# Expert rows by accumulating scatters instead of two fetched planes, in a two-layer graph and mixture-of-experts kernel

## The chip, the cores and the metric

The kernel runs on one core of one Trainium2 chip. The metric is the device time of one execution in microseconds (us), as the median of several runs. The core has five engines with queues of their own: TensorE (PE, and PEld for its weight loads), VectorE (DVE), ScalarE (ACT), GpSimd (POOL) and SyncE (SP), and 16 DMA engines that they share.

## What is computed

The reference adds four blocks to a residual `x` of 8192 tokens (64 groups of 128, in 4-byte floats) with 128 features each:

```
x = x + gnn0(layernorm(x))     # graph filter in the eigenbasis of the Laplacian
x = x + ffn0(layernorm(x))     # 8 experts, each token goes to 2 of them
x = x + gnn1(layernorm(x))     # graph filter with two batch norms
x = x + ffn1(layernorm(x))     # a shared expert, and 8 private ones, 2 of them for each token
```

Each of the two expert layers gives a token a weighted sum of two experts' rows:

```
gates = einsum('nk,nke->ne', topk_probs, onehot)
out   = einsum('ne,nec->nc', gates, y)
```

## The kernel before, in words

The code numbers the expert layers 0 and 1. The text calls them the first and the second one.

`X` holds the residual in SBUF, one partition for 64 tokens (token = 64 * partition + q), and is worked on in 16 slices of 4 values of q (512 tokens, 256 KB). Each layer of experts has two phases.

- Routing runs inside the graph stage before it. GpSimd scatters each token's normalized row twice, once for each expert chosen, into `rows` (`xs` in the code) in memory, with the gate and the token's number in two more columns (`Router.scatter`, L868).
- The experts then work on tiles of 256 rows of one expert. There are always `NT` = 71 tiles for each layer: 16384 rows, and padding of whole tiles. SyncE loads a tile (`experts_sp`, L1139), TensorE turns it, multiplies and turns it back in two halves of 128 rows, ScalarE writes half 0 times its gate to `ysb` (L1223) and VectorE half 1 (L1184). GpSimd sends each half to memory with one indirect DMA (`experts_pool`, L1150), so there are 142 of them for each layer. `ysb` has three buffers: both writers wait, for tile j, until the two scatters of tile j-3 have landed (`tile_back0` to `tile_back2`).

The destinations are in `goal`. It is filled with `NOWHERE`, a row that lies outside, and VectorE copies the token's number over it for real rows (L1172), so padding rows are dropped. In the number a token's second choice counts 8192 more than its first, so the two rows of a token land in two planes of 4 MB each (`planes`). No two scatters write the same bytes, and none waits for another.

After the last tile SyncE waits for all scatters and fetches the planes slice by slice into eight buffers (`fetch_planes`, L1329), and VectorE adds the two pieces to `X` (`add_planes`, L1338 and L1340). After the first expert layer this is the head of each step of `mix_dve`, in front of the layer norm sums (L926) of the next graph stage. After the second layer it is `last_dve`, and `last_store` on GpSimd writes each finished slice to `out` (L1642).

The order of the work is written by hand for each engine, and semaphores tie the engines together. SyncE's queue has, in this order: the loads of the start, the tile loads of the first layer, the second layer's weights (4.6 MB, L1765 and L1766, once the last tile of the first layer has copied its weights), the planes, the tile loads of the second layer, and the planes again.

Of the kernel before, what the change touches and what calls it, by code (L numbers as in the profile page):

```python
# [5 lines left out]
F32 = mybir.dt.float32  # L6
# [6 lines left out]
N = 64  # L13
# [671 lines left out]
ROW = P + 2  # L685
NOWHERE = 1 << 20
WB = (2 * HID0 + 3 * P, 2 * CH1 * P + CH1 + 2)
# [69 lines left out]
class Router:  # L757
# [115 lines left out]
    def table(self, dve, own):  # L873
# [187 lines left out]
def gnn0_dve(nc, dve, own, S, t, ps, route):  # L1061
    V, X = nc.vector, t["X"]
    dve.wait_ge(S("cleared"), 16 * BLOCKS)
    for s in range(A0_STEPS):
# [27 lines left out]

def clear_rows(nc, pool, S, zeros, xs):
# [7 lines left out]
    pool.wait_ge(S("cleared"), 16 * BLOCKS)  # L1101


def gnn0_pool(nc, pool, S, t, route, xs):
    for k in range(2):
        nc.gpsimd.iota(t["payi"][k][:, :, P], pattern=[[1, N]], base=k * TOKENS, channel_multiplier=N
                       ).then_inc(S("ids"), 1)
    pool.wait_ge(S("ids"), 2)

    def ready(g):  # L1110
        pool.wait_ge(S("a0_dup"), 2 * g + 2)
    for g in range(GROUPS):
        route.scatter(pool, g, xs, ready)


def uses(slot, ways):

    return len(range(slot, NT, ways))
# [23 lines left out]

def experts_pool(nc, pool, S, t, layer, planes):
# [174 lines left out]

def fetch_planes(sp, S, t, planes, layer, used):


    for w in range(3):
        sp.wait_ge(S(f"tile_back{w}"), 32 * uses(w, 3) * (layer + 1))
    rows = planes.rearrange("(k p q) c -> k p q c", k=2, p=P)
    for T in range(TILES):
        if T >= 8:
            sp.wait_ge(used, T - 7)
        for k in range(2):
            sp.dma_start(t["yb"][T % 8][:, k, :, :], rows[k][:, T * PAIRS:(T + 1) * PAIRS, :]  # L1329
                         ).then_inc(S(f"plane{T % 8}"), 16)  # L1330


def add_planes(V, dve, S, t, layer, T, done):

    xt = t["X"][:, T * PAIRS:(T + 1) * PAIRS, :]
    yb = t["yb"][T % 8]
    dve.wait_ge(S(f"plane{T % 8}"), 64 * layer + 32 * (T // 8 + 1))
    V.tensor_tensor(xt, xt, yb[:, 0, :, :], ALU.add).then_inc(done, 1)  # L1338
    dve.wait_ge(done, 2 * T + 1)
    V.tensor_tensor(xt, xt, yb[:, 1, :, :], ALU.add).then_inc(done, 1)  # L1340
    dve.wait_ge(done, 2 * T + 2)

# [272 lines left out]
def gnn1_pool(nc, pool, S, t, route, xs):  # L1615
    pool.wait_ge(S("bn2_ready"), 1)
    for k in range(2):
        nc.gpsimd.iota(t["payi"][k][:, :, P], pattern=[[1, N]], base=k * TOKENS, channel_multiplier=N
                       ).then_inc(S("ids"), 1)
# [8 lines left out]
def last_dve(nc, dve, S, t):  # L1628
    V = nc.vector
    for T in range(TILES):  # L1630
        if T == 0:
            dve.wait_ge(S("a1_xsh"), TILES)
        add_planes(V, dve, S, t, 1, T, S("z_add"))
        V.nop().then_inc(S("z_used"), 1)


def last_store(pool, S, t, out):

    for T in range(TILES):
        qs = slice(T * PAIRS, (T + 1) * PAIRS)  # L1640
        pool.wait_ge(S("z_used"), T + 1)
        pool.dma_start(out[:, qs, :], t["X"][:, qs, :]).then_inc(S("stored"), 16)  # L1642
    pool.wait_ge(S("stored"), 16 * TILES)


def build(nc, d, out, scratch):

    with ExitStack() as ctx:
# [8 lines left out]
        xs, planes = scratch  # L1657
        ps = [ctx.enter_context(nc.psum_tensor(f"bank{i}", [P, 512], F32)) for i in range(8)]
# [18 lines left out]
        t["OUT1"] = U1[:, :]  # L1677
        t["yb"] = [U1[:, w * 2 * TOK:(w + 1) * 2 * TOK].rearrange("p (k q c) -> p k q c", k=2, q=PAIRS) for w in range(8)]
        t["WS"] = W[:, E8 * WB[1]:E8 * WB[1] + WSH]
# [72 lines left out]
        def _(sp):  # L1752
# [8 lines left out]
            sp.dma_start(K[:, :], d["kroute"]).then_inc(S("kroute_in"), 16)  # L1761
            sp.dma_start(W[:, 0:E8 * WB[0]], d["w0"]).then_inc(S("w0_in"), 16)
            experts_sp(nc, sp, S, views[0], 0, xs)
# [3 lines left out]
            fetch_planes(sp, S, t, planes[0], 0, S("m_used"))  # L1767
            experts_sp(nc, sp, S, views[1], 1, xs)
            sp.wait_ge(S("a1_t1"), TILES)
            fetch_planes(sp, S, t, planes[1], 1, S("z_used"))  # L1770

# [14 lines left out]
        def _(dve):  # L1786
# [15 lines left out]
            experts_dve(nc, dve, own, S, views[1], ps, 1)  # L1802
            last_dve(nc, dve, S, t)

# [12 lines left out]
        @block.gpsimd  # L1817
        def _(pool):
            clear_rows(nc, pool, S, PAY[:, 0:ZERO], xs)
            gnn0_pool(nc, pool, S, t, routes[0], xs)  # L1820
            experts_pool(nc, pool, S, views[0], 0, planes[0])
            gnn1_pool(nc, pool, S, t, routes[1], xs)
            experts_pool(nc, pool, S, views[1], 1, planes[1])
            last_store(pool, S, t, out)

# [46 lines left out]
```

## Time and profile before

| what | value |
|---|---|
| median of 3 runs | 1550.68 us (1549.52 to 1550.79) |
| profiled execution, device time | 1551.85 us |
| its span, first to last instruction | 1550.1 us |
| busy: PE, DVE, ACT, POOL | 72%, 57%, 48%, 36% |
| mean DMA rate over the span | 81 GB/s |
| mean granted TensorE clock | 0.918 of full speed |

The profile is of one execution. Line numbers are those of the kernel before. Busy shares are means over stages with different limits: the stretches in which TensorE is full are those of the two expert layers, and the last 42 us have no TensorE work in them. Times to landing count from the start of the issuing instruction to the last update of the DMA's semaphore.

### The profile page before, as it was taken

What the parts mean: (1) busy time and instruction counts of PE and PEld (TensorE: products, weight loads), DVE (VectorE), ACT (ScalarE), POOL (GpSimd) and SP (SyncE); (2) the same over time, 40 slices, a digit from 0 to 9 for tenths busy, and PEclk for the clock granted to TensorE, in tenths of its full rate; (3) what the DMA queues carried; (4) which work ended last, traced back from release to release, by engine and by line L of the source; (5) the groups of instructions that cost most, each with busy time, mean ns of one, the idle gap of its engine ahead of it and who ended that gap; (6) DMA issues with size and microseconds to landing.
All of it is one profiled execution on the core that took longest, in us unless ns stands there. A gap on an engine that the chain in (4) does not pass through costs nothing.

```text
span 1550.1 us, 22393 instructions
## 1 busy us (share of the span) xinstructions
PE 1122.8 (72%) x5462; PEld 855.4 (55%) x5462; DVE 881.3 (57%) x3280; ACT 743.1 (48%) x2097; POOL 564.5 (36%) x575
## 2 busy tenths in 40 slices
PE   3445478028873049999999766859999499999970
PEld 3444467025652037777777533345554388888860
DVE  5555578866886026666666488686652233333325
ACT  3777748103451013443344367627775266666640
POOL 2000000000777744444444400006777455555543
PEclk9999999999895569999999989959999699999995
DMA  9991000000111111122222450001111122222218
GB/s 236 428 430 70 2 1 1 0 0 1 48 52 52 48 48 59 58 62 61 59 59 63 161 203 1 0 1 46 52 53 49 52 69 67 69 68 64 67 54 309
DMA packets 59120, 124.86 MB, mean 81 GB/s; under 512 B 13116, under 2 KB 39620, under 8 KB 57456
## 3 DMA queue, kind: packets, MB, share of 16 engines
q0 software_dynamic: 20000, 73.21, 12.7%
q1 hardware_dynamic: 38992, 50.23, 11.3%
q8 instruction: 45, 0.74, 0.2%
q14 instruction: 83, 0.68, 0.1%
HBM read 50.22 MB, written 74.99 MB: 81 GB/s over the span
## 4 chain that ended last, share of the span: by engine, by line
PE 57%; DVE 17%; ACT 8%; issue 7%; POOL 7%; DMA 3%; SPq 1%; DVEq 0%; POOLq 0%; ACTq 0%
PE bank L1289 14%; PE bank L1281 8%; POOL rows L868 7%; PE bank L1278 6%; PE bank L1279 6%; PE bank L366 3%; PE bank L1487 2%; PE bank L1480 2%; PE bank L181 2%; PE bank L1266 2%; PE bank L1300 2%; PE bank L1454 2%; DMA u<-planes 1%; ACT work L1394 1%; PE bank L1415 1%
## 5 line engine op out<-in xcount | busy, mean ns | idle before, releaser
L1150 POOL DMA_INDIRECT planes<-pay,goal x284 | 288.0, 1014 | 328.6 <-DVE pay L1184 152.5
L868 POOL DMA_INDIRECT rows<-pay,slot x256 | 252.1, 985 | 384.9 <-issue 348.7
L1289 PE MATMUL bank<-pay 128*128 128x256 f32 (+1 forms) x994 | 269.4, 388 | 0.1
L1167 DVE COPY pay<-wreg 128x1066 f32 (+1 forms) x142 | 111.7, 787 | 253.0 <-ACT pay L1249 107.0
L1289 PEld LDWEIGHTS bank<-pay 128*128 128x128 f32 (+1 forms) x994 | 173.0, 191 | 34.5 <-DVE pay L1203 17.0
L1235 ACT ACTIVATE pay<-bank 128x256 f32<-128x256 f32 (+1 forms) x213 | 81.6, 383 | 179.7 <-PE bank L1279 165.3
L1281 PE MATMUL bank<-pay 128*128 128x256 f32 x568 | 147.7, 383 | 0.6 <-DVE pay L1177 0.6
L1239 ACT ACTIVATE pay<-bank,pay 128x256 f32<-128x256 f32 x284 | 128.7, 474 | 26.7 <-PE bank L1281 26.7
L1278 PE MATMUL bank<-pay 128*128 128x256 f32 (+1 forms) x426 | 128.4, 383 | 0.6 <-DVE pay L1177 0.6
L1279 PE MATMUL bank<-pay 128*128 128x256 f32 (+1 forms) x426 | 128.0, 382 | 0.0
L181 PE MATMUL bank<-consts,u 63*64 63x1 f32 (+61 forms) x372 | 60.4, 274 | 89.7 <-DVE u L167 88.9
L1203 DVE TENSOR_TENSOR pay<-pay,bank 128x256 f32<-128x256 f32 (+1 forms) x213 | 88.6, 416 | 56.4 <-ACT pay L1235 55.7
L1266 PE MATMUL bank<-consts,pay 128*128 128x128 f32 x284 | 55.1, 276 | 84.3 <-DMA pay<-rows 84.3
L1281 PEld LDWEIGHTS bank<-pay 128*128 128x128 f32 x568 | 103.5, 192 | 12.4 <-issue 1.0
L181 PEld LDWEIGHTS bank<-consts,u 63*64 63x64 f32 (+61 forms) x372 | 51.2, 215 | 95.1 <-DVE u L167 94.1
L1177 DVE COPY pay<-bank 128x256 f32<-128x256 f32 x142 | 59.6, 419 | 66.8 <-PE bank L1266 66.7
L1266 PEld LDWEIGHTS bank<-consts,pay 128*128 128x128 f32 x284 | 40.3, 143 | 99.2 <-DMA pay<-rows 84.8
L1279 PEld LDWEIGHTS bank<-pay 128*128 128x128 f32 (+1 forms) x426 | 76.4, 179 | 16.8 <-issue 0.3
L1249 ACT ACTIVATE pay<-bank,pay 128x256 f32<-128x256 f32 x71 | 33.7, 474 | 105.0 <-PE bank L1289 105.0
L1278 PEld LDWEIGHTS bank<-pay 128*128 128x128 f32 (+1 forms) x426 | 68.3, 179 | 13.9 <-issue 1.1
L1487 PE MATMUL bank<-work,wreg 128*128 128x512 f32 x128 | 66.3, 620 | 5.2 <-ACT work L1542 5.0
L1247 ACT COPY pay<-bank 128x256 f32<-128x256 f32 x71 | 26.4, 373 | 88.3 <-PE bank L1289 88.3
(389 smaller groups left out, 2166.5 us busy)
## 6 DMA issues: line engine op xcount, KB each, us to landing
rows<-pay POOLq DMA_DIRECT2D x10, 3432.0 KB, 55.6
pay<-rows SPq DMA_DIRECT2D x142, 130.0 KB, 2.1
u<-planes SPq DMA_DIRECT2D x64, 256.0 KB, 6.4
planes<-pay,goal POOLq DMA_INDIRECT x284, 2.3
wreg<-in_w SPq DMA_DIRECT2D x1, 4264.0 KB, 24.9
wreg<-in_w SPq DMA_DIRECT2D x1, 4120.0 KB, 12.5
X<-in_x SPq DMA_DIRECT2D x2, 2048.0 KB, 20.5
rows<-pay,slot POOLq DMA_INDIRECT x256, 2.3
```

Of the source, the lines that this page charges most:

```text
L181: T.matmul(out, A[0:rows, col:col + 1].to_broadcast([rows, N]), rhs, start=True, stop=True).then_inc(hp, 1)
L868: self.nc.gpsimd.indirect_dma_start(out=xs, out_offset=bass.IndirectOffsetOnAxis(ap=self.t["slot"][:, k, q:q + 1], axis=0), in_=self.t["pa ...
L1150: nc.gpsimd.indirect_dma_start(out=planes, out_offset=bass.IndirectOffsetOnAxis(ap=t["goal"][:, j * 2 + h:j * 2 + h + 1], axis=0), in_=t[" ...
L1167: V.tensor_copy(t["wst"][j % 2][:, 0:WB[layer]], W[:, bass.ds(off, WB[layer])]).then_inc(s("w"), 1)
L1203: V.tensor_tensor(t["hh"][c][0:w, :], t["hs"][c][0:w, :], ps[c][0:w, TS:2 * TS], ALU.mult).then_inc(s("hh"), 1)
L1239: A.activation(t["hh"][c], ps[c][:, 0:TS], ACT.Gelu, bias=t["wst"][j % 2][:, 2 * CH1 * P + c:2 * CH1 * P + c + 1]).then_inc(s("hh"), 1)
L1266: ins = T.transpose(ps[6][:, h * P:(h + 1) * P], t["xin"][j % 4][:, h * ROW:h * ROW + P], t["ident"])
L1278: T.matmul(ps[c][0:n, 0:TS], w[:, a:a + n], x, start=True, stop=True)
L1279: T.matmul(ps[c][0:n, TS:2 * TS], w[:, HID0 + a:HID0 + a + n], x, start=True, stop=True).then_inc(s("up"), 1)
L1281: T.matmul(ps[c][:, 0:TS], w[:, c * P:(c + 1) * P], x, start=True, stop=True).then_inc(s("up"), 1)
L1289: ins = T.matmul(ps[7][:, 0:TS], t["wst"][j % 2][0:n, at + c * P:at + (c + 1) * P], t["hh"][c][0:n, :], start=(c == 0), stop=(c == n_c - 1))
L1487: T.matmul(ps[4][:, :], t["WS"][:, (CH1 + c) * P:(CH1 + c + 1) * P], t["sh"][c % 2], start=(c == 0), stop=(c == CH1 - 1)).then_inc(S("a1_d ...
```

## The change

The expert rows are added in memory, to a copy of the residual, by scatters with `compute_op=ALU.add`. For the second layer this copy is the output tensor itself.

- Before the experts' tile loads SyncE writes the 16 slices of `X` to memory (`keep_rows`): to `between` in the first layer and to `out` in the second. It waits for the instruction that finished each slice. GpSimd's first scatter of a layer waits for all of them (`x_kept`).
- Token numbers no longer carry the plane: both choices of a token go to the same row. GpSimd waits, before the first scatter of each tile, until both scatters of the tile before have landed, since two tiles may add to the same row.
- Padding rows go to 256 spare rows behind the 8192, one row for each place in a tile. They are cleared at the start; `goal` is filled by one `iota`, and the `memset` of `goal` is gone.
- After the first layer SyncE fetches the 16 slices of `between` straight into `X` (`fetch_rows`), and `mix_dve` starts with the norm sums. After the second layer nothing follows: `last_dve`, `last_store` and the second fetch are gone, and GpSimd waits for the last scatters (`all_back`).
- The output has the order of the tokens and is put in the reference's shape on the host.

```diff
-        own.chain(V.memset(self.t["goal"], NOWHERE))
+        dve.wait_ge(S("spare_rows"), 1)
...
+    for rows in sums:
+        pool.dma_start(rows[TOKENS:TOKENS + TS, :].rearrange("(p h) c -> p (h c)", h=2), zeros[:, 0:2 * D]
+                       ).then_inc(S("cleared"), 16)
...
+    nc.gpsimd.iota(spare, pattern=[[0, 2 * NT], [1, 2]], base=TOKENS, channel_multiplier=2).then_inc(S("spare_rows"), 1)
     for k in range(2):
-        nc.gpsimd.iota(t["payi"][k][:, :, P], pattern=[[1, N]], base=k * TOKENS, channel_multiplier=N
+        nc.gpsimd.iota(t["payi"][k][:, :, P], pattern=[[1, N]], base=0, channel_multiplier=N
...
+    pool.wait_ge(S("x_kept"), 16 * TILES * (layer + 1))
     for j in range(NT):
         pool.wait_ge(s("goal"), past("goal", j + 1))
+        if j >= 1:
+            before = f"back{(j - 1) % 3}"
+            pool.wait_ge(s(before), past(before, 32 * ((j - 1) // 3 + 1)))
         for h in range(2):
             pool.wait_ge(s(f"ys{h}"), past(f"ys{h}", j + 1))
             nc.gpsimd.indirect_dma_start(
-                out=planes, out_offset=bass.IndirectOffsetOnAxis(ap=t["goal"][:, j * 2 + h:j * 2 + h + 1], axis=0),
-                in_=t["ysb"][j % 3][:, h, :], in_offset=None, bounds_check=2 * TOKENS - 1, oob_is_err=False,
+                out=sums, out_offset=bass.IndirectOffsetOnAxis(ap=t["goal"][:, j * 2 + h:j * 2 + h + 1], axis=0),
+                in_=t["ysb"][j % 3][:, h, :], in_offset=None, bounds_check=TOKENS + TS - 1, oob_is_err=True,
+                compute_op=ALU.add,
             ).then_inc(s(f"back{j % 3}"), 16)
...
+def keep_rows(sp, S, t, sums, added):
+
     for T in range(TILES):
+        qs = slice(T * PAIRS, (T + 1) * PAIRS)
+        sp.wait_ge(added, T + 1)
+        sp.dma_start(by_place(sums)[:, qs, :], t["X"][:, qs, :]).then_inc(S("x_kept"), 16)
+
+
+def fetch_rows(sp, S, t, sums):
+
+    all_back(sp, S, 0)
+    for T in range(TILES):
+        qs = slice(T * PAIRS, (T + 1) * PAIRS)
         if T >= 8:
-            sp.wait_ge(used, T - 7)
...
+            sp.wait_ge(S("m_var"), T - 7)
+        sp.dma_start(t["X"][:, qs, :], by_place(sums)[:, qs, :]).then_inc(S(f"back_in{T % 8}"), 16)
...
-            add_planes(V, dve, S, t, 0, s, S("m_add"))
-            V.nop().then_inc(S("m_used"), 1)
+            dve.wait_ge(S(f"back_in{s % 8}"), 16 * (s // 8 + 1))
```

On GpSimd's queue, where the tiles of the first layer begin, stood this (`rows<-pay,slot` is the routing's scatter; the semaphores waited for are in brackets):

```order
L868 DMA rows<-pay,slot 67584x130 x15
L1150 DMA planes<-pay,goal 16384x128 [waits tile_ys0,tile_goal]
L1150 DMA planes<-pay,goal 16384x128 [waits tile_ys1]
L1150 DMA planes<-pay,goal 16384x128 [waits tile_ys0,tile_goal]
L1150 DMA planes<-pay,goal 16384x128 [waits tile_ys1]
```

In the changed kernel the same place reads:

```order
L867 DMA rows<-pay,slot 67584x130 x15
L1157 DMA between<-pay,goal 8448x128 [waits tile_ys0,tile_goal,x_kept]
L1157 DMA between<-pay,goal 8448x128 [waits tile_ys1]
L1157 DMA between<-pay,goal 8448x128 [waits tile_ys0,tile_back0,tile_goal]
L1157 DMA between<-pay,goal 8448x128 [waits tile_ys1]
L1157 DMA between<-pay,goal 8448x128 [waits tile_ys0,tile_back1,tile_goal]
L1157 DMA between<-pay,goal 8448x128 [waits tile_ys1]
```

No instruction moved, but the first scatter of each tile from the second on has one more wait: `tile_back` of the tile just before. The second scatter of a tile waits for nothing new.

On SyncE's queue, from the second layer's weights to the first tile loads of the second layer and then at the end, stood this (`ints` is the table of a tile's first row):

```order
L1765 DMA wreg<-in_w 128x8240 [waits tile_w]
L1766 DMA wreg<-in_ws 128x1029
L1329 DMA u<-planes 128x512 [waits tile_back2,tile_back1,tile_back0]
L1329 DMA u<-planes 128x512 x15
...
L1329 DMA u<-planes 128x512 [waits tile_back1,tile_back2,tile_back0,a1_t1]
L1329 DMA u<-planes 128x512 x15
```

In the changed kernel the first of these places reads as follows, and at the end nothing stands behind the tile loads:

```order
L1757 DMA wreg<-in_w 128x8240 [waits tile_w]
L1758 DMA wreg<-in_ws 128x1029
L1352 DMA X<-between 128x512 [waits tile_back2,tile_back1,tile_back0]
L1352 DMA X<-between 128x512 x7
L1352 DMA X<-between 128x512 [waits m_var] x8
L1342 DMA out<-X 128x512 [waits a1_xsh] x16
L1136 TENSOR_LOAD ints [waits route_first,route_sent]
```

The fetches are halved to 16, the residual's stores stand ahead of the second layer's tile loads, and the fetches behind the second layer are gone.

## Rows read from the trace of the kernel before

**Rows 1.** Windows: busy us (instructions) by engine, granted clock, DMA share, GB/s.
```profile
core 0: us, PE busy (x) PEld busy (x) DVE busy (x) ACT busy (x) POOL busy (x), PEclk, DMA share, GB/s
574.00:885.00 311.00, 307.62 (x1526) 241.94 (x1524) 189.55 (x484) 125.29 (x349) 147.77 (x142) 1.00 0.23 71
1232.00:1506.00 274.00, 270.85 (x1390) 234.66 (x1388) 100.18 (x275) 168.44 (x418) 138.66 (x142) 1.00 0.22 65
1508.00:1550.00 42.00, 0.00 (x0) 0.00 (x0) 22.14 (x32) 0.00 (x0) 12.15 (x16) 0.50 0.82 300
893.00:974.00 81.00, 53.17 (x192) 28.36 (x192) 68.15 (x241) 54.63 (x128) 0.00 (x0) 0.93 0.26 91
```

**Rows 2.** Timeline of GpSimd, at three places: start, duration, idle before.
```profile
574.39 0.98 POOL L1150 DMA_INDIRECT planes<-pay,goal  x1 [16.34 <-DVE pay L1184]
...
1232.46 0.98 POOL L1150 DMA_INDIRECT planes<-pay,goal  x1 [14.53 <-DVE goal L1172]
...
1399.94 0.98 POOL L1150 DMA_INDIRECT planes<-pay,goal  x1 [1.63 <-DVE goal L1172]
1401.22 0.98 POOL L1150 DMA_INDIRECT planes<-pay,goal  x1 [0.30 <-issue]
1403.83 0.98 POOL L1150 DMA_INDIRECT planes<-pay,goal  x1 [1.62 <-DVE goal L1172]
```

**Rows 3.** Line L1150, from 560 to 890 us: durations in ns, landings.
```profile
L1150 POOL DMA_INDIRECT planes<-pay,goal x142: 977/980/1359, 574.4 to 884.7; - x142
...
DMA to landing us min/median/max: 2.1/2.3/8.9
```

**Rows 4.** The chain that ended last, end of the first expert layer: start, us, what.
```profile
882.17 0.38 ACT pay L1223
882.55 0.02 issue
882.57 0.02 POOLq L1149
...
883.37 0.98 POOL planes L1150
884.35 0.30 issue
884.65 3.53 DMA planes<-pay,goal
...
888.61 2.96 DMA u<-planes
...
891.60 0.70 DVE X L1338
```

**Rows 5.** The same chain, end of the kernel.
```profile
1504.65 0.98 POOL planes L1150
1505.63 0.30 issue
1505.94 2.10 DMA planes<-pay,goal
```

**Rows 6.** DMA issues from 560 to 886 us: count, KB each, median us to landing.
```profile
pay<-rows SPq DMA_DIRECT2D x71, 130.0 KB, 2.1
wreg<-in_w SPq DMA_DIRECT2D x1, 4120.0 KB, 12.5
```

**Rows 7.** Line L1150, from 874 to 880 us: landings.
```profile
DMA to landing us min/median/max: 7.7/8.3/8.9
```

**Rows 8.** The chain from 910 to 930 us.
```profile
914.48 1.27 ACT pay L1386 x2
915.75 0.67 ACT work L1394 x2
...
917.33 1.17 PE bank L1415 x8
...
919.01 1.27 ACT pay L1386 x2
```

**Rows 9.** VectorE's last additions to X ahead of either layer's experts.
```profile
L1088 DVE TENSOR_TENSOR X<-X,bank x12: 686/688/689, 383.5 to 470.0; 128x512 f32<-128x512 f32 x12
L1612 DVE TENSOR_TENSOR X<-X,bank x16: 687/689/690, 1064.1 to 1200.0; 128x512 f32<-128x512 f32 x16
```

More of the change, by code:

```diff
@@ L685 @@
 ROW = P + 2
-NOWHERE = 1 << 20
 WB = (2 * HID0 + 3 * P, 2 * CH1 * P + CH1 + 2)
@@ L1062, in gnn0_dve @@
     V, X = nc.vector, t["X"]
-    dve.wait_ge(S("cleared"), 16 * BLOCKS)
+    dve.wait_ge(S("cleared"), 16 * (BLOCKS + 2))
     for s in range(A0_STEPS):
@@ L1090, in gnn0_dve, with clear_rows @@
             norm_sums(V, dve, own, t, xt, S("a0_var"))
-def clear_rows(nc, pool, S, zeros, xs):
+def clear_rows(nc, pool, S, zeros, xs, sums):
     nc.gpsimd.memset(zeros, 0.0).then_inc(S("zeros"), 1)
@@ L1100, in clear_rows, with gnn0_pool @@
         pool.dma_start(blocks[n], zeros).then_inc(S("cleared"), 16)
-    pool.wait_ge(S("cleared"), 16 * BLOCKS)
-def gnn0_pool(nc, pool, S, t, route, xs):
+    for rows in sums:
+        pool.dma_start(rows[TOKENS:TOKENS + TS, :].rearrange("(p h) c -> p (h c)", h=2), zeros[:, 0:2 * D]
+                       ).then_inc(S("cleared"), 16)
+    pool.wait_ge(S("cleared"), 16 * (BLOCKS + 2))
+def gnn0_pool(nc, pool, S, t, route, xs, spare):
+    nc.gpsimd.iota(spare, pattern=[[0, 2 * NT], [1, 2]], base=TOKENS, channel_multiplier=2).then_inc(S("spare_rows"), 1)
     for k in range(2):
-        nc.gpsimd.iota(t["payi"][k][:, :, P], pattern=[[1, N]], base=k * TOKENS, channel_multiplier=N
+        nc.gpsimd.iota(t["payi"][k][:, :, P], pattern=[[1, N]], base=0, channel_multiplier=N
                        ).then_inc(S("ids"), 1)
@@ L1140, in experts_sp, with experts_pool @@
                      ).then_inc(s(f"xin{j % 4}"), 16)
-def experts_pool(nc, pool, S, t, layer, planes):
+def experts_pool(nc, pool, S, t, layer, sums):
     s = lambda n: S(f"tile_{n}")
     past = lambda name, n: FIRST_LAYER[name] * layer + n
+    pool.wait_ge(S("x_kept"), 16 * TILES * (layer + 1))
     for j in range(NT):
         pool.wait_ge(s("goal"), past("goal", j + 1))
+        if j >= 1:
+            before = f"back{(j - 1) % 3}"
+            pool.wait_ge(s(before), past(before, 32 * ((j - 1) // 3 + 1)))
         for h in range(2):
@@ L1316, in experts_pe, with by_place, all_back @@
     turn_back(NT - 1)
-def fetch_planes(sp, S, t, planes, layer, used):
+def by_place(sums):
+    return sums[0:TOKENS, :].rearrange("(p q) c -> p q c", p=P)
+def all_back(eng, S, layer):
     for w in range(3):
-        sp.wait_ge(S(f"tile_back{w}"), 32 * uses(w, 3) * (layer + 1))
-    rows = planes.rearrange("(k p q) c -> k p q c", k=2, p=P)
+        eng.wait_ge(S(f"tile_back{w}"), 32 * uses(w, 3) * (layer + 1))
+def keep_rows(sp, S, t, sums, added):
     for T in range(TILES):
-        if T >= 8:
-            sp.wait_ge(used, T - 7)
[L1328 to L1341, printed above, removed]
+        qs = slice(T * PAIRS, (T + 1) * PAIRS)
[5 more added lines that the diff above has]
+        qs = slice(T * PAIRS, (T + 1) * PAIRS)
+        if T >= 8:
+            sp.wait_ge(S("m_var"), T - 7)
+        sp.dma_start(t["X"][:, qs, :], by_place(sums)[:, qs, :]).then_inc(S(f"back_in{T % 8}"), 16)
 MIX_STEPS = TILES + 3
@@ L1617, in gnn1_pool @@
     for k in range(2):
-        nc.gpsimd.iota(t["payi"][k][:, :, P], pattern=[[1, N]], base=k * TOKENS, channel_multiplier=N
+        nc.gpsimd.iota(t["payi"][k][:, :, P], pattern=[[1, N]], base=0, channel_multiplier=N
                        ).then_inc(S("ids"), 1)
@@ L1625, in gnn1_pool, with build @@
         route.scatter(pool, g, xs, ready)
[L1628 to L1646, printed above, removed]
+def build(nc, d, scratch):
     with ExitStack() as ctx:
@@ L1656, in S @@
             return sems[name]
-        xs, planes = scratch
+        xs, sums = scratch
         ps = [ctx.enter_context(nc.psum_tensor(f"bank{i}", [P, 512], F32)) for i in range(8)]
@@ L1677, in build @@
         t["OUT1"] = U1[:, :]
-        t["yb"] = [U1[:, w * 2 * TOK:(w + 1) * 2 * TOK].rearrange("p (k q c) -> p k q c", k=2, q=PAIRS) for w in range(8)]
         t["WS"] = W[:, E8 * WB[1]:E8 * WB[1] + WSH]
@@ L1762, in _ @@
             sp.dma_start(W[:, 0:E8 * WB[0]], d["w0"]).then_inc(S("w0_in"), 16)
+            keep_rows(sp, S, t, sums[0], S("a0_xadd"))
             experts_sp(nc, sp, S, views[0], 0, xs)
@@ L1766, in _ @@
             sp.dma_start(t["WS"], d["ws"]).then_inc(S("w1_in"), 16)
-            fetch_planes(sp, S, t, planes[0], 0, S("m_used"))
+            fetch_rows(sp, S, t, sums[0])
+            keep_rows(sp, S, t, sums[1], S("a1_xsh"))
             experts_sp(nc, sp, S, views[1], 1, xs)
-            sp.wait_ge(S("a1_t1"), TILES)
-            fetch_planes(sp, S, t, planes[1], 1, S("z_used"))
         @block.tensor
@@ L1802, in _ @@
             experts_dve(nc, dve, own, S, views[1], ps, 1)
-            last_dve(nc, dve, S, t)
         @block.scalar
@@ L1818, in _ @@
         def _(pool):
-            clear_rows(nc, pool, S, PAY[:, 0:ZERO], xs)
-            gnn0_pool(nc, pool, S, t, routes[0], xs)
-            experts_pool(nc, pool, S, views[0], 0, planes[0])
+            clear_rows(nc, pool, S, PAY[:, 0:ZERO], xs, sums)
+            gnn0_pool(nc, pool, S, t, routes[0], xs, goal[:, :, :].rearrange("p l (j h) -> p (l j) h", h=2))
+            experts_pool(nc, pool, S, views[0], 0, sums[0])
             gnn1_pool(nc, pool, S, t, routes[1], xs)
-            experts_pool(nc, pool, S, views[1], 1, planes[1])
-            last_store(pool, S, t, out)
+            experts_pool(nc, pool, S, views[1], 1, sums[1])
+            all_back(pool, S, 1)
 def kernel(x, adj, L0_gnn_W1, L0_gnn_b1, L0_gnn_W2, L0_gnn_b2, L0_ffn_router_w, L0_ffn_w1, L0_ffn_w2, L0_ffn_w3,
@@ L1865 @@
     d = {k[3:]: nc.dram_tensor(k, v.shape, F32, kind="ExternalInput").ap() for k, v in arrays.items()}
-    out = nc.dram_tensor("out", (N, P, D), F32, kind="ExternalOutput").ap()
+    out = nc.dram_tensor("out", (TOKENS + TS, D), F32, kind="ExternalOutput").ap()
     xs = nc.dram_tensor("rows", (E8 * CAP, ROW), F32).ap()
-    planes = [nc.dram_tensor(f"planes{n}", (2 * TOKENS, D), F32).ap() for n in range(2)]
-    build(nc, d, out.rearrange("q r d -> r q d"), (xs, planes))
+    between = nc.dram_tensor("between", (TOKENS + TS, D), F32).ap()
+    build(nc, d, (xs, (between, out)))
     r = run_bass_kernel_spmd(nc, [arrays], core_ids=[0])
-    return r.results[0]["out"].reshape(2 * N, N, D)
+    rows = r.results[0]["out"][0:TOKENS]
+    return np.ascontiguousarray(rows.reshape(2, N, N, D).transpose(2, 0, 1, 3).reshape(2 * N, N, D))
```

## The prediction

> **What bounds the kernel now.** I read the windows first. In both expert layers TensorE is busy 307.62 of 311 us and 270.85 of 274 us at full clock, with the DMA engines at 0.22 to 0.23 of their time: these stages run at TensorE's pace [rows 1]. From 1508 to 1550 us TensorE does nothing and the DMA engines move 300 GB/s: this is the fetch, the additions and the stores of the planes [rows 1].
>
> Then I read GpSimd's scatters. In the first layer the first halves of tile 0 and tile 70 start at 574.39 and 883.37 us [rows 2, 4], so a tile takes 308.98 / 70 = 4.41 us. In the second layer they start at 1232.46 and 1504.65 us [rows 2, 5], which gives 272.19 / 70 = 3.89 us. GpSimd is busy for 2 x 0.98 us of each tile and waits for VectorE or ScalarE in the rest [rows 2]. It has slack in issuing. But a scatter takes 2.3 us to land in the median, counted from its start [rows 3], and nobody waits for that until three tiles later. The change makes the next tile wait for it. So the question is how long a tile takes when it is a closed loop through the landing.
>
> **The loop of one tile, after.** Its steps, and their rows:
> - Release to start of the instruction: ScalarE ends at 882.55 and the scatter begins at 883.37 us, 0.82 us [rows 4]. GpSimd prepares nothing ahead of a wait, so this is paid each time. I take the same for a release by a DMA.
> - First scatter to second: 1504.65 to 1505.94, 1.29 us [rows 5].
> - Landing of the second scatter, L, from its start.
>
> So the loop is C = 0.82 + 1.29 + L = 2.11 + L. With the plain scatter's 2.3 us it is 4.41 us: just the pace of the first layer, and 0.52 us more than that of the second.
>
> **What L is.** No accumulating DMA is in this trace. Each of its rows has to be read from memory, added, and written. From below it can't beat the plain scatter of the same bytes, 2.1 to 2.3 us [rows 3]. From above, a read from memory that lands before a write to memory starts would be pay<-rows (130 KB, 2.1 us) [rows 6] and then the scatter, 2.3 us: 4.4 us. Both parts hold the fixed cost of a DMA, which is probably not paid twice in full, and neither holds the addition or a longer descriptor list, which could also stretch the 0.98 us of the instruction (each 0.1 us of it counts twice in a tile, since the landing is counted from the start). Neither end is nearer to a row of the same kind, so I take the middle: L = 3.3 us, C = 5.41 us. The new form with a bounds error in place of a dropped row has no row either, and is inside that spread.
>
> The Trainium skill ("DMA: Bandwidth & Descriptors", section "Anatomy of one DMA — SWDGE (gpsimd) path") fits a GpSimd DMA as 2.0 us plus its bytes over 436 GB/s, most of it the write receipt, and names no price for accumulating. For these 64 KB this is an estimate of 2.15 us, which agrees with the 2.1 to 2.3 us of the trace. By that fit C would be 4.26 us and the whole kernel near 1531 us: that is the rival on the other side, worked out from rows below. The same page (section "Rules for kernel authors") says that an accumulate reads its destination and writes it later with nothing held in between, so the wait for the earlier semaphore can't be left out. No run here shows this yet.
>
> **First layer.** 70 x 5.41 = 378.7 us in place of 309.0: +69.7 us. The last landing was slow, 3.53 us, because the second layer's weights were being loaded [rows 4]; the same slot costs 3.3 now: -0.2 us. These weights have a cost of another kind. They are asked for when the last tile copies its weights, and land after 12.5 us [rows 6]; the scatters that start meanwhile need 7.7 to 8.9 us [rows 7]. Before, only the fetch waited, for the last of them. In the loop, a tile then takes some 2.1 + 8.3 = 10.4 us, and 12.5 us hold about 1.2 such tiles, each 5 us longer than C: +6 us.
>
> **The stage behind it (mix).** The first fetched slice is needed once instead of twice, and the first pair of additions falls away: they are on the chain, from 891.60 to 893.06 us or two times 0.7 [rows 4], and half the bytes land perhaps 0.5 us sooner: -2 us. The other 30 additions (0.69 us each) are worth nothing: a step lasts 919.01 - 914.48 = 4.53 us and its chain goes through ScalarE and TensorE alone [rows 8], with VectorE beside it. If that cover were gone, they would give up to 21 us.
>
> **Ahead of the experts.** The residual's 16 stores per layer, 4.2 MB, stand on SyncE's queue where it otherwise waits for the routing's last scatters. The last slices are ready near 470 and 1200.7 us [rows 9], and the first scatter starts at 574.39 and 1232.46 us [rows 2]. At the 300 GB/s of the tail [rows 1] all 16 take 14 us, so more than 30 us cover them: 0. Without cover they would cost up to 14 us in a layer. The tile loads behind them on the queue wait for the routing anyway. Two clears of 128 KB at the start, one iota against one memset, and the removed empty instructions: 0, all off the chain. The 1792 padding rows of a layer that are now written add a ninth to bytes that take under a quarter of the DMA engines.
>
> So the first layer and what surrounds it shift the second by 69.7 - 0.2 + 6 - 2 = +73.5 us.
>
> **Second layer and end.** Without the shift, the first scatter starts at 1232.46 us; the last one has landed at 1232.46 + 378.7 + 1.29 + 3.3 = 1615.8 us, and nothing follows. Before, the span ended at 1550.1 us. So +65.7 us: the removed tail of 42.1 us (1508.04 to 1550.1) [rows 1, 5] is more than eaten by 70 x (5.41 - 3.89) = 106 us, and the landing is 1.2 us longer.
>
> **Sum.** 1550.1 + 73.5 + 65.7 = 1689.3 us of span. The profiled execution took 1.75 us more than its span and stands 1.17 us above the median of the runs, so as a median: 1690 us.
>
> In general one more 0.1 us in L or in C gives 142 x 0.1 = 14 us. The break-even is where 140C + 2L = 624.9 us, L = 2.32 us: the median of the plain scatter. A chain of accumulating scatters must be as fast as plain ones only to lose nothing.
>
> **Rivals.**
> - *The accumulating scatter lands as soon as the fastest plain one.* For it: the DMA engines are idle for three quarters of the time, and one scatter is 4 KB for each of 16 engines. Against it: the extra read. At L = 2.1 us, C = 4.21: the first layer stays at TensorE's pace (-3 us with the mix), and the second ends at 1232.46 + 294.7 + 1.29 + 2.1 = 1530.6 us, -19.5. Together 1528 us. It is faster only for L under 2.3 us. Chance 0.07, and 0.02 for a draw, L from 2.30 to 2.34 us. Were the loop hidden wholly, with C under 3.89 us, it would be 1506 us; 0.82 + 1.29 us before any landing leaves 1.78 us for L, less than any landing seen. I give it 0.01 of the 0.07.
> - *The rows of a scatter go one after another.* Each DMA engine has 8 rows of it, and if read and write of one row must end before the next begins, the extra grows several times. Twice the bound's excess over the plain scatter (2 x 2.1 us) gives L = 6.5 and C = 8.6 us: 1690 + 142 x 3.2 = 2144 us. Nothing in the trace excludes it for this kind of DMA; plain reads overlap, since 130 KB of them land in 2.1 us [rows 6]. Chance of L over 4.8 us: 0.08.
> - *TensorE's clock falls.* With C = 5.4 us TensorE is busy 3.9 of 5.4 us, 72%, in the second layer. The mix stage has 53.17 of 81 us and was granted 0.93 [rows 1], so I expect little. If both layers ran at half clock, a tile would need 7.8 to 8.8 us of TensorE, about 2100 us. Chance 0.02.
> - *A landing of 2.34 to 2.43 us*, a small loss, 1553 to 1565 us: chance 0.01.
> - *The forecast, L of 2.43 to 4.8 us*: chance 0.80. The sum gives 1690 - 142 x 0.87 = 1566 us at 2.43, and 142 x 1.5 = 213 us above 1690, near 1900, at 4.8. The bounds 2.3 and 4.4 themselves give 1548 and 1846 us.
>
> The range is 1565 to 1900 us; it leaves out 0.10 below and 0.10 above. A change under 0.2%, 3 us, can't be told from none. Faster 0.07, same 0.02, slower 0.91.
>
> **What the changed profile would show.** Right: GpSimd's idle time before the first scatter of a tile is ended by the DMA of the tile before, not by VectorE or ScalarE; first halves start at equal distances in both layers, near 5.4 us, the same for both though their TensorE work differs; TensorE's busy share falls to about 80% and 72% there; the landing of the accumulating scatter is 3.3 us and that of single ones near the weights' load 8 us; the last instruction is a scatter, and the tail of 42 us is gone. Wrong: the two layers keep different paces (then TensorE still bounds), or the scatter instruction itself is much over 0.98 us (then descriptors cost, not landing), or the granted clock in the layers is well below 1.

## The result, and the profile after

The changed kernel takes 1811.1 us (median of 4 runs, 1808.76 to 1816.33), the kernel before 1550.1 us, now the median of four runs: 1.169 times as long, 95% interval 1.166 to 1.172. That is 261 us more, where 140 us were forecast. One execution of one experiment below, the weights asked for later, ran at a granted clock of 0.63 and took 2073 us; it is left out of every figure.

The windows of the changed kernel, in the columns of [rows 1], over the first expert layer, the second one and the mix stage:

```profile
574.00:1034.00 460.00, 339.12 (x1523) 256.79 (x1521) 187.36 (x484) 124.93 (x348) 245.17 (x142) 0.92 0.33 51
1375.00:1806.00 431.00, 303.94 (x1389) 239.31 (x1387) 100.45 (x275) 169.74 (x417) 222.88 (x142) 0.94 0.32 43
1041.00:1120.00 79.00, 52.20 (x190) 27.39 (x189) 46.54 (x190) 54.48 (x126) 0.00 (x0) 0.95 0.09 25
```

TensorE, full before, is busy 74% and 71% of the two layers, and they last 460 and 431 us in place of 311 and 274 [rows 1]. GpSimd is busy for only half of that time, so neither engine is full: the layers are bound by a wait. The timeline of GpSimd shows it, first in the first layer, then in the second, and then the last scatters of the kernel:

```profile
700.65 1.55 POOL L1157 DMA_INDIRECT between<-pay,goal  x1 [2.57 <-DVE pay L1192]
702.50 2.00 POOL L1157 DMA_INDIRECT between<-pay,goal  x1 [0.30 <-issue]
707.01 1.55 POOL L1157 DMA_INDIRECT between<-pay,goal  x1 [2.51 <-DVE pay L1192]
...
1564.81 1.55 POOL L1157 DMA_INDIRECT out<-pay,goal  x1 [2.62 <-DVE goal L1180]
1566.66 1.55 POOL L1157 DMA_INDIRECT out<-pay,goal  x1 [0.30 <-issue]
1570.89 1.55 POOL L1157 DMA_INDIRECT out<-pay,goal  x1 [2.67 <-DVE goal L1180]
...
1802.36 1.55 POOL L1157 DMA_INDIRECT out<-pay,goal  x1 [2.48 <-issue]
1804.21 1.55 POOL L1157 DMA_INDIRECT out<-pay,goal  x1 [0.30 <-issue]
```

The instruction takes 1.55 us where it took 0.98 [rows 2], and 2.00 us in many second halves of the first layer. A tile takes 6.36 us at the first place and 6.08 at the second. The releaser named in the brackets is misleading: VectorE and ScalarE are themselves waiting for a landing here. In both layers the first scatter of a tile starts 0.8 us after the second one of the tile before has landed, which is the release term of the forecast. The summary of the line shows who waited: durations in ns, then who waited for its landings (us, times; both layers together), then the landings:

```profile
L1157 POOL DMA_INDIRECT between<-pay,goal x142: 1547/1552/2095, 573.8 to 1030.0; - x142
L1157 POOL DMA_INDIRECT out<-pay,goal x142: 1547/1549/1960, 1375.2 to 1804.2; - x142
...
  ACT pay L1231: 314.5, 128
  DVE pay L1192: 299.7, 125
...
DMA to landing us min/median/max: 3.2/3.3/13.6
```

The writers of `ysb` waited 128 and 125 times for a scatter to land, where the same summary of the kernel before names nobody: all three buffers are full, and GpSimd is the one that is late. The landing is 3.3 us in the median over both layers, against 2.3 [rows 3]; the second scatters of the first layer, which close its loop, have 3.7 us.

The stretch in which the second layer's weights are loaded (asked for at 990.93 us), and the hand-over to the mix stage:

```profile
988.46 1.55 POOL L1157 DMA_INDIRECT between<-pay,goal  x1 [2.44 <-DVE pay L1192]
990.31 2.00 POOL L1157 DMA_INDIRECT between<-pay,goal  x1 [0.30 <-issue]
1004.69 1.55 POOL L1157 DMA_INDIRECT between<-pay,goal  x1 [12.37 <-DVE pay L1192]
...
1028.10 1.55 POOL L1157 DMA_INDIRECT between<-pay,goal  x1 [2.49 <-issue]
1029.96 1.55 POOL L1157 DMA_INDIRECT between<-pay,goal  x1 [0.30 <-issue]
1033.18 3.65 SPq L1352 DMA_DIRECT2D X<-between  x8
1035.93 0.68 DVE L925 BATCH_NORM_STATS2 bn<-X 128x6 f32<-128x128 f32 x3 [19.90 <-DMA X<-between]
```

One scatter landed after 13.6 us and made one tile 16.2 us long. The last landing of the layer is at 1033.1 us, and the norm sums follow 2.8 us later, with no additions ahead of them.

### The profile page after: what moved, and what is told of

Its sections match the earlier page's. It is cut to its first block and busy times, and to the rows that moved or that the text cites. A ratio compares the mean times of both kernels' runs of the same rounds, so it can differ in the third digit from the quotient of the medians.

```text
span 1810.5 us, 22264 instructions
## 1 busy us (share of the span) xinstructions
PE 1191.7 (66%) x5462; PEld 878.3 (49%) x5462; DVE 836.4 (46%) x3214; ACT 744.3 (41%) x2097; POOL 734.4 (41%) x562
## 3 DMA queue, kind: packets, MB, share of 16 engines
q0 software_dynamic: 50624, 71.09, 19.0%
## 5 line engine op out<-in xcount | busy, mean ns | idle before, releaser
L1297 PE MATMUL bank<-pay 128*128 128x256 f32 (+1 forms) x994 | 302.3, 402 | 208.0 <-ACT pay L1247 108.1
L1157 POOL DMA_INDIRECT between<-pay,goal x142 | 245.3, 1728 | 228.7 <-DVE pay L1192 183.2
L1157 POOL DMA_INDIRECT out<-pay,goal x142 | 222.9, 1570 | 222.2 <-DVE goal L1180 173.1
L1297 PEld LDWEIGHTS bank<-pay 128*128 128x128 f32 (+1 forms) x994 | 169.6, 193 | 276.3 <-ACT pay L1247 133.9
L1175 DVE COPY pay<-wreg 128x1066 f32 (+1 forms) x142 | 101.1, 712 | 277.7 <-ACT pay L1257 129.2
L1192 DVE TENSOR_SCALAR pay<-bank,pay 128x128 f32<-128x128 f32 x142 | 49.8, 350 | 299.7 <-DMA out<-pay,goal 182.2
L1231 ACT ACTIVATE pay<-bank,pay 128x128 f32<-128x128 f32 x142 | 52.1, 367 | 314.5 <-DMA out<-pay,goal 171.0
L1289 PE MATMUL bank<-pay 128*128 128x256 f32 x568 | 158.1, 405 | 0.6 <-DVE pay L1185 0.6
L1286 PE MATMUL bank<-pay 128*128 128x256 f32 (+1 forms) x426 | 139.4, 411 | 0.6 <-DVE pay L1185 0.6
L1287 PE MATMUL bank<-pay 128*128 128x256 f32 (+1 forms) x426 | 138.4, 409 | 0.0
L1247 ACT ACTIVATE pay<-bank,pay 128x256 f32<-128x256 f32 x284 | 124.4, 473 | 32.9 <-PE bank L1289 32.9
L1289 PEld LDWEIGHTS bank<-pay 128*128 128x128 f32 x568 | 110.8, 206 | 14.8 <-issue 1.0
L1287 PEld LDWEIGHTS bank<-pay 128*128 128x128 f32 (+1 forms) x426 | 83.2, 195 | 20.2 <-issue 1.8
L1286 PEld LDWEIGHTS bank<-pay 128*128 128x128 f32 (+1 forms) x426 | 74.1, 193 | 15.3 <-issue 1.5
```

The source lines that it names most:

```text
L1157: nc.gpsimd.indirect_dma_start(out=sums, out_offset=bass.IndirectOffsetOnAxis(ap=t["goal"][:, j * 2 + h:j * 2 + h + 1], axis=0), in_=t["ys ...
L1175: V.tensor_copy(t["wst"][j % 2][:, 0:WB[layer]], W[:, bass.ds(off, WB[layer])]).then_inc(s("w"), 1)
L1247: A.activation(t["hh"][c], ps[c][:, 0:TS], ACT.Gelu, bias=t["wst"][j % 2][:, 2 * CH1 * P + c:2 * CH1 * P + c + 1]).then_inc(s("hh"), 1)
L1286: T.matmul(ps[c][0:n, 0:TS], w[:, a:a + n], x, start=True, stop=True)
L1287: T.matmul(ps[c][0:n, TS:2 * TS], w[:, HID0 + a:HID0 + a + n], x, start=True, stop=True).then_inc(s("up"), 1)
L1289: T.matmul(ps[c][:, 0:TS], w[:, c * P:(c + 1) * P], x, start=True, stop=True).then_inc(s("up"), 1)
```

## The experiments

Layer paces are taken from the first halves of tiles 0 and 70, as in the forecast. The experiments ran in two later batches in which the kernel before took 1548.2 us (the first four) and 1547.7 us (the other four); each ratio is against the one of its own batch. The changed kernel was not run again in them, so differences to its 1811.1 us are uncertain by the 2 us between the batches.

**Plain scatters in the chain.** The wait stays and the addition is left out.

```diff
-                compute_op=ALU.add,
```

> The changed kernel with plain scatters in place of accumulating ones; everything else, the wait for the tile before included, stays. It leaves out the additions, so the sums are wrong. Theory A (a tile is a closed loop of 0.82 us release, two scatter instructions 0.3 us apart, and the landing, and the addition lengthens both the instruction, 0.98 to 1.55 us, and the landing): the instruction goes back to 0.98 us and the landing to 2.3 us, the loop to 4.4 us, so both layers run at 4.4 to 4.5 us for a tile and the kernel takes 1540 to 1556 us. Rival B (the form that reports a row out of bounds is what makes the instruction 1.55 us long): it stays at 1.55 us, the loop is 5.3 us or more, the time 1670 us or more. Rival C (a release by a DMA's landing costs more than the 0.82 us of a release by an engine): a loop of over 4.7 us, 1590 us or more.

Measured: 1575.0 us (1562 to 1579), 1.016 times the kernel before (1.010 to 1.022). The bounds error form is still there. One tile of each layer on GpSimd, and the summary of the line:

```profile
703.65 1.05 POOL L1157 DMA_INDIRECT between<-pay,goal  x1 [2.09 <-issue]
705.00 0.98 POOL L1157 DMA_INDIRECT between<-pay,goal  x1 [0.30 <-issue]
708.06 1.07 POOL L1157 DMA_INDIRECT between<-pay,goal  x1 [2.08 <-issue]
...
1400.65 0.98 POOL L1157 DMA_INDIRECT out<-pay,goal  x1 [2.10 <-DVE goal L1179]
1401.93 0.98 POOL L1157 DMA_INDIRECT out<-pay,goal  x1 [0.30 <-issue]
1405.02 0.98 POOL L1157 DMA_INDIRECT out<-pay,goal  x1 [2.11 <-DVE goal L1179]
...
DMA to landing us min/median/max: 2.2/2.3/7.8
```

The undisturbed loop is 4.37 to 4.41 us, as 0.82 + 1.29 + 2.3 says, and the instruction is back at 0.98 us: the addition makes it 1.55 us, not the bounds form (rival B is out). From a landing to the start of the next scatter it is 0.82 to 0.84 us in the median, so a release by a DMA costs what another one does (rival C is out). But the time is 19 us above the expected interval. The paces are 4.78 and 4.50 us on average. In the first layer 23 tiles have a second scatter of about 1.26 us in place of 0.98, because VectorE's copy of the next weights runs beside it; most of these tiles take 4.6 us. Other tiles take 5 to 6.6 us and one, beside the weights, 9.9. A closed loop pays for each late landing, and the middle value of one tile does not show these.

No run was made to find what makes single landings late, but the trace shows what goes with them. This scatter landed after 3.9 us; the last two lines are the DMA queues between its start and its landing (packets, MB, share):

```profile
1525.25 1.10 POOL L1157 DMA_INDIRECT out<-pay,goal  x1 [0.30 <-issue]
1530.00 0.98 POOL L1157 DMA_INDIRECT out<-pay,goal  x1 [3.66 <-DVE goal L1179]
...
q0 software_dynamic: 64, 0.13, 10.2%
q8 instruction: 1, 0.02, 2.0%
```

A packet of a kind that the profile calls "instruction" moved meanwhile. The two scatters beside the weights aside, that is so for all 15 landings of over 3.2 us in this trace, though only 81 of 282 landings have such a packet; in the changed kernel it is so for all 9 of over 4.2 us, with 85 of 283. That the packet is the cause is not shown; no run has one without the other.

So the chain alone, with plain scatters, already eats the removed tail of 42 us and 27 us more (1575.0 against 1548.2 us).

**Accumulating scatters without the chain.** In the kernel before, with both planes cleared at the start.

```diff
                 in_=t["ysb"][j % 3][:, h, :], in_offset=None, bounds_check=2 * TOKENS - 1, oob_is_err=False,
+                compute_op=ALU.add,
...
+    for both in planes:
+        parts = both.rearrange("r c -> (r c)").rearrange("(n p x) -> n p x", p=P, x=4096)
+        for n in range(4):
+            pool.dma_start(parts[n], zeros[:, 0:4096]).then_inc(S("cleared"), 16)
```

> The kernel before with accumulating scatters into its two planes, which are cleared at the start; each row of a plane gets one addend, so no scatter waits for another. Theory A: the instruction takes 1.55 us and the landing 3.3 us, but two instructions with their gaps are 3.7 us, under the 3.89 and 4.41 us of a tile on TensorE, and nobody waits for the landing: 1548 to 1556 us. Rival D (accumulating costs time by itself, through GpSimd or the DMA engines, without the wait): GpSimd's instruction stretched to 2 us as in the first layer of the changed kernel would need 4.15 us for a tile, 18 us more over the second layer, 1568 us, or more if DMAs of other queues are slowed.

Measured: 1552.95 us, 1.0027 times (1.0015 to 1.0038), 2 to 6 us more than before. GpSimd in the second layer, and the windows of both layers:

```profile
1400.53 1.74 POOL L1154 DMA_INDIRECT planes<-pay,goal  x1 [0.30 <-issue]
1402.57 1.55 POOL L1154 DMA_INDIRECT planes<-pay,goal  x1 [0.30 <-issue]
1404.43 1.74 POOL L1154 DMA_INDIRECT planes<-pay,goal  x1 [0.30 <-issue]
1406.47 1.55 POOL L1154 DMA_INDIRECT planes<-pay,goal  x1 [0.30 <-issue]
...
574.00:885.00 311.00, 306.51 (x1520) 241.14 (x1519) 181.11 (x481) 123.28 (x346) 249.10 (x140) 1.00 0.46 72
1234.00:1510.00 276.00, 270.81 (x1390) 234.70 (x1388) 100.09 (x275) 168.34 (x417) 226.76 (x142) 0.99 0.47 64
```

In the second layer GpSimd is just about full (3.9 us for a tile) and TensorE's pace holds. The landing, 3.7 us in the median of the first layer and 3.4 us in the second, costs nothing when nobody waits for it. One tile at the end of the first layer takes 7.5 us: the scatters beside the weights' load land after up to 11.7 us, and there the writers do wait once for a buffer. The addition by itself is nearly free; rival D is out. Inside the chain the same addition costs 236 us (1811.1 against 1575.0 us of the chain with plain scatters), since there the longer instruction and the later landing are waited for.

**A wait for the tile two before.** Even tiles go to one tensor, odd ones to another, which is cleared at the start and left out of the sums, so the output lacks half of the experts' rows. The traffic stays.

```diff
-        if j >= 1:
-            before = f"back{(j - 1) % 3}"
-            pool.wait_ge(s(before), past(before, 32 * ((j - 1) // 3 + 1)))
+        if j >= 2:
+            before = f"back{(j - 2) % 3}"
+            pool.wait_ge(s(before), past(before, 32 * ((j - 2) // 3 + 1)))
...
-                out=sums, out_offset=bass.IndirectOffsetOnAxis(ap=t["goal"][:, j * 2 + h:j * 2 + h + 1], axis=0),
+                out=sums[j % 2], out_offset=bass.IndirectOffsetOnAxis(ap=t["goal"][:, j * 2 + h:j * 2 + h + 1], axis=0),
```

> The changed kernel with even tiles added to one tensor and odd tiles to another one (cleared at the start), and each tile waiting for the landing of the tile two before it. The odd tensor is left out of the sums, so half of the experts' rows are missing in the output. Theory A: a loop through two tiles, 0.82 + 1.85 + 3.3 = 6.0 us for both, 3.0 us for one, is shorter than TensorE's 3.89 us, and GpSimd needs 3.7 us: both layers are back at TensorE's pace, the tail of 42 us stays away, 1505 to 1512 us; up to 1530 us if GpSimd's instruction is stretched in the second layer. Rival D (accumulating itself is slow): paces stay well above 4.4 and 3.9 us, over 1600 us.

Measured: 1519.0 us, 0.981 times (0.979 to 0.983). Both layers are back at TensorE's pace, 4.43 and 3.89 us in most tiles. GpSimd in the second layer, and beside the weights' load in the first:

```profile
1399.78 1.55 POOL L1161 DMA_INDIRECT out<-pay,goal  x1 [0.30 <-issue]
1401.63 1.74 POOL L1161 DMA_INDIRECT out<-pay,goal  x1 [0.30 <-issue]
1403.67 1.55 POOL L1161 DMA_INDIRECT other<-pay,goal  x1 [0.30 <-issue]
...
873.65 1.55 POOL L1161 DMA_INDIRECT between<-pay,goal  x1 [0.51 <-DVE pay L1196]
875.50 1.55 POOL L1161 DMA_INDIRECT between<-pay,goal  x1 [0.30 <-issue]
885.56 1.55 POOL L1161 DMA_INDIRECT other<-pay,goal  x1 [8.51 <-ACT pay L1235]
```

It misses the 1505 to 1512 us by 7 us, which is one tile of 11.9 us beside the weights' load in the first layer, 7.5 us over the pace; that term had been left out of the expectation. The distance of the wait is worth 292 us of the changed kernel's time: that is the cause.

**The weights asked for later.**

```diff
+            fetch_rows(sp, S, t, sums[0])
             sp.wait_ge(S("tile_w"), NT)
             sp.dma_start(W[:, 0:E8 * WB[1]], d["w1"]).then_inc(S("w1_in"), 16)
             sp.dma_start(t["WS"], d["ws"]).then_inc(S("w1_in"), 16)
-            fetch_rows(sp, S, t, sums[0])
```

> The changed kernel with the second layer's weights (4.6 MB) asked for behind the fetch of the residual instead of during the last tiles of the first layer. Theory A: the one tile of 16.2 us (its scatter landed after 13.6 us beside these weights) becomes one of 5.9 us, and the weights land long before the shared expert needs them: 10 us less than the changed kernel, 1798 to 1804 us. Rival E (the stall comes back in the fetch or in the wait for the weights): 1808 us or more.

Measured: 1799.8 us (median of three runs, 1799.3 to 1803.1), 11 us less than the changed kernel. In the trace no landing of the first layer is over 4.7 us, the tile of 16.2 us is gone, and the 71 tiles take 10 us less. Theory A holds.

**The copy of the weights moved in the first layer.**

```diff
-        if j + 1 < NT:
+        if j + 1 < NT and layer == 1:
             weights(j + 1)
...
+                if c == 0 and j + 1 < NT:
+                    weights(j + 1)
```

> The changed kernel with VectorE's copy of the next tile's weights in the first layer moved behind its first product. In the changed kernel this copy runs when the second scatter of a tile starts, and that instruction takes 2.0 us instead of 1.55 us in 51 of 71 tiles. Theory F (the copy stretches the scatter instruction and with it the loop): the instruction is 1.55 us in nearly all tiles, the loop of the first layer 5.9 us instead of 6.4 us, 25 to 35 us less than the changed kernel, 1776 to 1788 us. Rival G (the stretch comes from something else, or the copy meets the instruction again in its new place): 1800 us or more.

Measured: 1787.2 us (1782 to 1797), 24 us less: inside 1776 to 1788 us, though just short of the 25 to 35 us less that were expected. In the changed kernel the copy is running when the second scatter starts; here it starts 1.4 us later. First the changed kernel, then this one:

```profile
702.37 0.72 DVE L1175 COPY pay<-wreg 128x1066 f32 x1 [0.95 <-ACT pay L1255]
702.50 2.00 POOL L1157 DMA_INDIRECT between<-pay,goal  x1 [0.30 <-issue]
```

```profile
701.95 1.55 POOL L1157 DMA_INDIRECT between<-pay,goal  x1 [0.30 <-issue]
703.35 0.72 DVE L1175 COPY pay<-wreg 128x1066 f32 x1 [0.40 <-issue]
706.01 1.55 POOL L1157 DMA_INDIRECT between<-pay,goal  x1 [2.51 <-DVE pay L1192]
```

The loop goes from 6.4 to 6.0 us in the median, and over-long second scatters from 51 to 3 of 71: 0.45 us of a stretched instruction are paid in full. The trace of this run has the whole 24 us in the first layer's pace, of which 3 us are a shorter tile beside the weights (13.6 us) that the edit does not aim at. So a copy of 0.72 us on an engine that is busy for 41% of the layer cost some 21 us. Theory F holds.

**The second layer alone.** The first layer is as before, with its planes, their fetch and their additions; the second one is that of the changed kernel.

> The first layer as before (two planes), the second one as in the changed kernel (chained accumulating scatters into the output). Theory A (the two layers' costs are separate and add up): the first scatter of the second layer starts near 1232.5 us as before, then 427 us of chain and 8 us to the end, 1668 us, 1660 to 1676 us. Rival H (part of the cost is shared, such as a lower clock or traffic from the residual's stores): outside of this, below 1650 or above 1690 us.

Measured: 1665.5 us, 1.076 times (1.074 to 1.079), inside 1660 to 1676 us. Against the 1547.7 us of its batch this is +118 us, the part of the second layer with its removed tail; the other 143 us belong to the first. The trace of the changed kernel gives the same two parts by itself, 117.7 and 142.7 us (see below), so nothing sizeable is shared between the layers.

**The wait only where it is needed.** Rows of one expert belong to different tokens, so two tiles can meet only where the expert changes, or in the spare rows. Every tile waits for the tile two before it, and the first tile of an expert for the one just before as well. SyncE does it ahead of time and passes it on with `go`; `gate` holds, for each tile, the count to wait for, made on VectorE behind the routing's table.

```diff
+    c[:, K_GATE] = [32 * uses((j - 1) % 3, 3) + 32 * ((j - 1) // 3) for j in range(P)]
...
+            own.chain(V.tensor_scalar(tb["m"], tb["start"], j, None, ALU.is_equal))
+            own.chain(V.scalar_tensor_tensor(out=tb["m"], in0=tb["end"], scalar=j, in1=tb["m"], op0=ALU.is_gt, op1=ALU.mult))
+            own.chain(V.tensor_reduce(tb["v"], tb["m"], AX.X, ALU.add))
...
+                V.tensor_scalar(self.t["gate"], tb["v"], 32.0, K[:, K_GATE:K_GATE + 1], ALU.mult, ALU.add).then_inc(S("gates_made"), 1)
...
+def open_gate(sp, S, t, g):
...
+    need = sp.value_load(t["gate"][g:g + 1, 0:1], min_val=32, max_val=2048)
+    sp.wait_ge(S(f"tile_{name}"), need)
+    sp.nop().then_inc(S("go"), 1)
...
-            before = f"back{(j - 1) % 3}"
-            pool.wait_ge(s(before), past(before, 32 * ((j - 1) // 3 + 1)))
+            pool.wait_ge(S("go"), j)
```

> As second_only, but a tile waits for the landing of the tile just before it only where it is the first tile of an expert (rows of one expert belong to different tokens); every tile waits for the tile two before it. SyncE does the waiting and passes it on, and spare rows alternate between two sets. Theory A (the cost is the chain, not the accumulation): seven to eight waits of 2 us each remain, partly made good by GpSimd, so the second layer takes 272 to 285 us and the kernel 1513 to 1530 us, below the kernel before. Rival D (accumulation or the added waiting on SyncE costs time in every tile): 1550 us or more.

Measured: 1525.7 us, 0.986 times the kernel before (0.984 to 0.988), 22 us less. It is the fastest kernel here that leaves nothing out. GpSimd at the first change of expert:

```profile
1257.75 1.55 POOL L1186 DMA_INDIRECT out<-pay,goal  x1 [0.49 <-issue]
1259.61 1.55 POOL L1186 DMA_INDIRECT out<-pay,goal  x1 [0.30 <-issue]
1261.65 1.55 POOL L1186 DMA_INDIRECT out<-pay,goal  x1 [0.49 <-issue]
1263.50 1.55 POOL L1186 DMA_INDIRECT out<-pay,goal  x1 [0.30 <-issue]
1267.86 1.90 POOL L1186 DMA_INDIRECT out<-pay,goal  x1 [2.81 <-issue]
```

Tiles are 3.9 us apart, and exactly seven of the 70 distances are 6.1 to 6.4 us, one for each change between eight experts. The first of them is that from 1261.65 to 1267.86 us. The removed tail is kept, less 7 x 2.3 = 16 us. Of the 42 us of the tail only 37 are saved: from the first scatter of the last tile it is now 8.3 us to the end of the span, where the last landing alone came 3.4 us after it before. 37 - 16 = 21 us, and 22 were measured.

**The same with the weights later.** The edit is that of the late weights.

> As gated_second, with the second layer's weights asked for behind the fetch of the planes. Theory A: the last scatters of the first layer land 1.2 us sooner and the first planes come sooner, since nothing shares the DMA engines with them: 0 to 6 us less than gated_second. Rival I (the weights now come while the planes or later loads need the DMA engines): the same or more.

Measured: 1526.7 us (1525.5 to 1528.2), the same as without it (1524.7 to 1528.5); theory A allowed 0, so the time does not tell it from rival I. The traces do in part: no scatter lands after more than 3.4 us in the first layer, and the mix stage's norm sums start at 890.1 us, 1.0 us sooner, as theory A says; but the second layer's first scatter comes at 1229.2 us, 2.6 us later. Rival I's reason for that is not seen, since the weights have landed by 939 us. Where the gain is lost stays open. With the first layer unchained there is little to gain: only the fetch waits for the slow landings.

## Why the prediction was right in its direction and short in its size

- **The closed loop** was right: release, two instructions, landing, 70 times in each layer, in place of TensorE's pace. The release term (0.8 us) is as forecast too. Three runs show the loop from three sides: the chain without the addition costs time, the addition without the chain does not, and the chain at distance two does not. The forecast's sign for it, a DMA named as the releaser of a tile's first scatter, did not come, since the writers wait for the same landings and are named in its place.
- **The landing** was forecast at 3.3 us, the middle between bounds of 2.1 and 4.4, and is 3.3 us. This is luck in part: the forecast had the excess over a plain scatter come from the read in memory, and more than half of it (0.57 of 1.0 us) is GpSimd's longer instruction.
- **The term that was too small** is "first scatter to second: 1.29 us". The accumulating instruction takes 1.55 us, and the term is 1.85 us. The forecast had said that a longer instruction would count twice, and then left it inside the spread of L, where it counts once. 0.56 us in 70 tiles of two layers are 78 us of the 121 missing. Of the forecast's signs of being wrong this one came: "the scatter instruction itself is much over 0.98 us".
- **The stretch of the instruction** to 2.0 us by VectorE's copy was not forecast; `copy_later` puts it at 21 to 24 us. It also is what made the two layers keep different paces, 6.49 and 6.10 us, the second sign of being wrong; that sign was read as "TensorE still bounds", and here it does not.
- **The weights' load** was taken as +6 us; the scatter landed after 13.6 us where 8.3 were said, the tile was 16.2 us long, and `late_weights` gives 10 us. The rest is some 15 us: 9 us are late landings in the second layer (its average tile is 6.10 us, where 0.82 + 1.85 + 3.3 is 5.97), 3 us are the end after the last landing, and about 3 us of the first layer are not assigned.
- By layer: the second layer's first scatter came at 1375.17 us, +142.7 where +73.5 was said [rows 2]; from there to the end it took 435.3 us, against 317.6 before, +117.7 where +65.7 was said.
- **The removed tail and the mix stage** went as forecast but for the end: after the last landing (1807.5 us) the span goes on for 3.1 us, which the forecast left out. From the last landing of the first layer to the second layer's first scatter it took 342.0 us, against 344.3 before [rows 2, 4]: -2.3 us, where -2 was said, and the 30 other additions were worth nothing.
- **The residual's stores** cost nothing, as forecast: the first scatter of each layer is released by VectorE, after 16.32 and 14.54 us of idle time, where it was 16.34 and 14.53 us before [rows 2].
- **TensorE's clock** was granted at 0.92 and 0.94 in layers with TensorE busy for 74% and 71%, where it was 1.00 when TensorE was full [rows 1]. That is the third sign of being wrong, "well below 1", in a mild form. It is not the bound: the buffers behind TensorE were full.
- The estimate by the Trainium skill ("DMA: Bandwidth & Descriptors", section "Anatomy of one DMA — SWDGE (gpsimd) path"), 2.15 us for 64 KB, agrees with the plain scatter here (2.2 to 2.3 us) and is 1.1 us short for the accumulating one. Half of what is missing is in GpSimd's instruction and not behind it: from its end, a plain scatter lands 1.3 us later and an accumulating one 1.7 us.

## What to carry to other kernels

Before a transfer that nobody waits for is put into a chain, write the loop down as release + instruction + landing, and compare it with the pace of the engine that bounds the stage: here 6.0 us against 3.9 and 4.4. The costs inside such a loop are paid in full each time, also those that were hidden before: a longer instruction, a copy that collides with it, a large load beside it. Ask then whether the wait is needed each time; here 7 of 70 were, and with these alone the second layer's part of the change is worth 22 us.

## What the runs showed of the hardware

- An accumulating scatter of 128 rows of 512 bytes keeps GpSimd for 1.55 us, against 0.98 us for a plain one, and lands 3.2 to 3.3 us after its start in quiet stretches, against 2.2 to 2.3 us (`after` and `plain_chained`).
- It doubles the time of the DMA engines: their share in the layers goes from 0.22 and 0.23 [rows 1] to 0.46 and 0.47 at the same pace (`acc_unchained`). A plain scatter moves in packets of 4096 bytes, an accumulating one in packets of 512, one for each row: for the same 71.09 MB GpSimd's queue has 50624 packets in the changed kernel and 18816 in the chain with plain scatters, and the difference is 112 (128 - 16) for each of the 284 scatters.
- A copy of VectorE (0.72 us) makes GpSimd's scatter instruction longer, but only at certain moments. Copies that were running when the accumulating instruction started made it up to 0.5 us longer (1.55 to 2.0 us in 51 tiles of the changed kernel). Copies that started up to 0.05 us after it did not: in the second layer that is so for 50 of them, and the instruction stays at 1.55 us. Copies that started 1.0 to 1.2 us after it did again (1.76 to 1.96 us, 4 times there), and those 1.4 us after it, as in `copy_later`, did not. In the chain with plain scatters a copy 0.43 us after the start makes 1.26 us of 0.98. So a shift of some 0.15 us between two engines decides whether a tile is 0.45 us longer.
- A scatter beside a 4.6 MB load of another queue landed after 13.6 us in the changed kernel, after up to 11.7 us in `acc_unchained` and after 7.8 us, as a plain one, in `plain_chained`.
- From a landing to the start of the scatter that waits for it GpSimd takes 0.80 to 0.84 us in the median (`after` and `plain_chained`); two scatters that wait for nothing are 0.30 us apart.
